# Expert gates as two f16 parts held twice, with one pass of bias products

## The chip, the cores and the metric

The kernel runs on one core of a Trainium2 chip. The metric is the device time of one execution in microseconds, as the median of several runs. The engines: TensorE (PE) multiplies matrices, VectorE (DVE), ScalarE (ACT) and GpSimd (POOL) work on SBUF and PSUM, SyncE (SP) issues the transfers. Each runs its own queue of instructions in order; they wait for each other by semaphores.

## The reference

Input x has the shape (16, 64, 112, 112). In short:

```python
v = _ln_c(x)                                   # norm over the channels
pooled = stack([max(v, axis=1), mean(v, axis=1)], axis=1)
x = x + v * sigmoid(conv3x3(pooled, conv_w) + conv_b)
t = _to_tokens(x)                              # tokens of 64 channels
u = _ln_t(t)                                   # norm of each token
probs = softmax(u @ router_w + router_b)       # 8 experts
top_p, top_i = top_k(probs, 2); top_p /= sum(top_p)
t = t + sum over the 2 of top_p * (u @ expert_w[i] + expert_b[i])
```

The affine steps of both norms and of the gate of the convolution reduce, for a token, to a few numbers: the gate of each expert, the same gate times the token's scale rho, the residual's scale and a mean term.

## The kernel before, in words

The 16 images go as 8 pairs (the two images lie on partitions 0 to 63 and 64 to 127). A pair has 14 steps of 8 image rows, 896 tokens an image. Three stages run at once on three different pairs, and a "round" r is the time in which stage A works on pair r, stage B on pair r - 1 and stage C on pair r - 2. Rounds 2 to 7 have all stages, round 8 has no stage A, rounds 9 and 10 only the rest of stage C. Each engine's order of work is written out by hand in its body(r, ...); the same step appears in each engine's queue.

- Stage A: TensorE centres the rows of x (centre_rows, L444, two groups a step). ScalarE copies the result to xct, squares it and sums; VectorE takes the maximum over the channels (L639).
- Stage B: the router and the gate. Its work has image row as partition (112 partitions). gate() puts one piece of it at each place 2 * step + late of VectorE: root_step (L751, L753, L756: two or more inputs in SBUF) at places 1 to 3 and 7 to 9, half_router at places 12 to 19 for the first half of the tokens and 20 to 27 for the second. At the third and seventh of these eight places stand key (L689) and key_max (L681), at the fourth oh1 (L697) and dl (L699). GpSimd has one or two operations of 896 elements in most steps (router, router_tail), among them e (L1237), that the root step of place 1 waits for, summed_gates (L1216) and scaled_gates (L1222).
- Stage C: the expert mixture in channel form, step v = step - 2. All numbers of a token are first split in bfloat16 parts so that TensorE can move them exactly, turned to rows of the matrix s (turn, L458), and spread over the channels by a matmul against a 0/1 matrix (spread, L465) into four PSUM banks gb. VectorE multiplies six of the eight spread gates by x (scale_unit, L662, gx<-gb,xd), GpSimd two of them (L1148), which ScalarE first copies out of PSUM (L963, gs). experts (L520) multiplies gx by the expert's weights and adds up in PSUM (moe); biases (L514) adds the bias of the chosen experts to the same accumulator. spread_a1 (L504) makes the scale of the residual, GpSimd multiplies it by x (tt, L1173), and VectorE adds tt and moe (finish, L675).

The parts: q holds for a token 18 numbers (8 scaled gates, 8 gates, 2 others). part_one (ScalarE, L942) rounds q to bfloat16, rest_one (GpSimd, L1156) subtracts it from q, part_two (ScalarE, L948) rounds the rest, part_three (GpSimd, L1162) subtracts again. The turn waits for part_three. Expert biases are split in two f16 parts, bh and bl, and each is multiplied with s in a pass of its own.

The order of one step on TensorE, with the calls before each wait on VectorE:

```
spread(v,1) spread_pool(v,1) | expert 5 of v-1 | turn(v+1) | biases(v,0) | expert 0
spread(v,2) spread(v,3) | centre_rows 0 | expert 1, pool expert 0
spread(v,4) spread_pool(v+1,0) | expert 2 | spread_a1(v+1) | biases(v,1) | expert 3
spread(v,5) spread(v+1,0) | centre_rows 1 | expert 4, pool expert 1
```

On VectorE a step is: gate(late=False), scale 1, finish, scale 2, scale 3, maximum, gate(late=True), scale 4, finish, scale 5, scale 0 of v+1, maximum. On GpSimd: scale_unit(v,1), rest_one(v+2), router pieces, scale_unit(v+1,0), scale_x (tt), part_three(v+2). A spread waits until VectorE has read the bank that it writes.

Of the kernel before, what the change touches and what calls it, by code (L numbers as in the profile page):

```python
# [33 lines left out]
E = 8  # L34
P = 128
# [19 lines left out]
SB = 64  # L55
SR = SB + 3 * QN
QG, QB, QA, QM = 0, E, 2 * E, 2 * E + 1
D_PAIR = (0, 1, 3, 0, 1, 3)
# [11 lines left out]
         + tuple(n + "_1" for n in HALF_ROUTER))  # L70
B_POOL = ("lg_0", "bias_0", "lg_1", "bias_1", "m1_0", "m2_0", "qb_0", "qg_0", "m1_1", "m2_1", "qb_1", "qg_1")
B_NORM = ("e1", "e2")
B_ACT = ("sig", "wide_0", "g1_0", "g2_0", "qa_0", "wide2_0", "wide_1", "g1_1", "g2_1", "wide2_1", "qa_1")
GUESS = 0x5F3759DF


def constant_arrays():

    f = np.zeros((P, CC + 3 * W + E + P), np.float32)
# [12 lines left out]
    f[:, o:o + E] = np.arange(E, 0, -1)  # L92
    o += E
    for part in range(3):
        for b in range(2):
            f[b * SB + part * QN + QM, o + b * CH:o + (b + 1) * CH] = -1.0
    g = np.zeros((P, (KT + 2) * P), np.float32)
    for part in range(3):
        for b in range(2):
            row = b * SB + part * QN  # L100
            for k in range(KT):
                for e in range(2):
                    lo = k * P + e * CH
                    g[row + QG + 2 * k + e, lo:lo + CH] = 1.0
            g[row + QA, KT * P + b * CH:KT * P + (b + 1) * CH] = 1.0
    g[:, (KT + 1) * P:] = np.eye(P)
    return f, g


def gated_expert_program(nc, x, conv_w, conv_b, router_w, router_b, expert_w, expert_b, const_f, const_g, out):  # L110
# [3 lines left out]
    with ExitStack() as ctx:  # L114
        def sb(name, shape, dt=F32):
            return ctx.enter_context(nc.sbuf_tensor(name, shape, dt))
# [4 lines left out]
        def sem(name):  # L121
            return ctx.enter_context(nc.semaphore(name))

        cf = sb("cf", [P, CC + 3 * W + E + P])
        cg = sb("cg", [P, (KT + 2) * P], BF16)
        gx = sb("gx", [P, UNITS, 2, HALF])
# [16 lines left out]
        bh = sb("bh", [SR, P], F16)  # L143
        bl = sb("bl", [SR, P], F16)
        cwb = sb("cwb", [W, 18])
# [39 lines left out]
        q = sb("q", [W, H, 2 * QN])  # L185
        res = sb("res", [W, 2, ROWS, 2 * QN])
        parts = sb("parts", [W, 2, ROWS, 2 * SB], BF16)
        s = sb("s", [P, 2, TOK], BF16)
        gs = sb("gs", [P, NP, 2, HALF])
# [9 lines left out]
        conv_out = tm[0:W, 0, 0:2 * H]  # L199
        turn_out = tm[:, 1, :].bitcast(BF16)  # L200

# [23 lines left out]
        rest1 = sem("rest1")  # L225
        part2 = sem("part2")
        part3 = sem("part3")
        turned = sem("turned")
# [11 lines left out]

        FIRST_LOADS, LOADS, BIAS_LOADS = 3 * 16, 5 * 16, 6 * 16
        POOL_SETUP = 5 + 1 + 6 * 5 + 1 + 2

# [16 lines left out]
        def c_at(r, per_step, v, n):  # L260
            return at(r, 2, per_step * STEPS, per_step * v + n)
# [72 lines left out]
        def _(sp):  # L334
# [65 lines left out]
            sp.wait_ge(ld_first, FIRST_LOADS)  # L400
            for part in range(3):
                for b in range(2):
                    row = b * SB + part * QN + QB
                    col = bias_c + b * CH
                    sp.dma_start(cf[row:row + E, col:col + CH], expert_b).then_inc(ld_bias, 16)

# [12 lines left out]
        def _(pe):  # L419
# [41 lines left out]

            def spread(v, k, c, slot):
                for b in range(2):
                    rows = slice(b * SB, b * SB + 3 * QN)
# [416 lines left out]
        def _(act):  # L881
# [168 lines left out]
            def body(r, A, Bp, steps=STEPS, tail=True):  # L1050
                for step in range(steps):
# [26 lines left out]
                    if A:  # L1078
                        square(r, step, 1)
                    if parting:  # L1080
                        part_two(r, v + 2)
                    if Bp and step == 8:
# [21 lines left out]
        def _(pool):  # L1104
# [171 lines left out]
            def body(r, Bp, steps=STEPS, tail=True):  # L1276
                for step in range(steps):
# [49 lines left out]
```

## Time and profile before

| | |
|---|---|
| median of 3 runs | 1491.57 us (1489.61 to 1493.1) |
| profiled execution, its own time | 1497.93 us |
| its span | 1496.1 us |
| TensorE busy | 1402.2 us, 94% |
| VectorE busy | 1268.4 us, 85% |
| ScalarE busy | 1080.0 us, 72% |
| GpSimd busy | 1086.4 us, 73% |
| mean granted clock of TensorE | 0.963 |

The time of a run is the whole execution; the span reaches from the first to the last instruction of the profile. Busy shares are averages over all rounds. A timeline row gives the start in us from the span's start, the duration in us, the engine and line, the operation, what it writes and reads, and in brackets the idle time of the engine before it with what ended it.

### The profile page before, as it was taken

The page shows a single profiled execution, that of the slowest core. Times are in us where ns is not written, and L with a number is a line of the kernel's source. Part 1 is how long each engine was busy: PE and PEld are TensorE (multiplying, and loading weights), DVE is VectorE, ACT ScalarE, POOL GpSimd, SP SyncE. Part 2 cuts the span into 40 slices and gives each one's busy share as a digit, 9 for nine tenths or more (in the row PEclk, how much of TensorE's full clock was granted, in tenths as well). Part 3 has the DMA queues.
Part 4 walks back from the last instruction along what each step waited for, and adds up shares of the span by engine and source line. Part 5 has one row for each costly group of instructions (what it writes and reads, how often), then busy time and mean ns, then how long its engine had stood idle before and what let it go on. Part 6 is the DMA issues. An engine that isn't in the chain of part 4 may idle for free.

```text
span 1496.1 us, 34317 instructions
## 1 busy us (share of the span) xinstructions
PE 1402.2 (94%) x12198; PEld 660.5 (44%) x12198; DVE 1268.4 (85%) x1583; ACT 1080.0 (72%) x4061; POOL 1086.4 (73%) x729
## 2 busy tenths in 40 slices
PE   8854999999999999999999999999999889999998
PEld 8853444444444444444444444444444233333332
DVE  6787889988998889988898889988898788977776
ACT  6667788878887888878888788878888334444432
POOL 5234687868777787877788687876878678887765
PEclk9955999999999999999999999999999899999999
DMA  6442466656666566666656666666665356556563
GB/s 221 125 114 60 138 197 197 203 156 203 190 188 193 178 199 197 185 179 193 185 173 198 186 186 192 177 199 186 195 193 169 101 151 170 173 164 182 165 181 112
DMA packets 85851, 260.04 MB, mean 174 GB/s; under 512 B 13744, under 2 KB 13744, under 8 KB 85680
## 3 DMA queue, kind: packets, MB, share of 16 engines
q1 hardware_dynamic: 85680, 257.85, 57.7%
q8 instruction: 97, 1.59, 0.4%
q14 instruction: 74, 0.61, 0.1%
HBM read 206.41 MB, written 51.38 MB: 172 GB/s over the span
## 4 chain that ended last, share of the span: by engine, by line
PE 69%; DVE 9%; issue 7%; POOL 3%; ACT 3%; DVEq 0%; POOLq 0%; ACTq 0%
PE moe L520 39%; PE gb L465 13%; PE tm L444 8%; DVE gx L662 7%; PE moe L514 4%; PE tm L458 3%; PE tm L504 2%; POOL gx L1148 1%; PE tm L544 1%; POOL tt L1173 1%; ACT a1s L970 1%; ACT sq L919 1%; POOL parts L1162 1%; DVE stats L639 0%; ACT logit_mean L985 0%
## 5 line engine op out<-in xcount | busy, mean ns | idle before, releaser
L662 DVE TENSOR_TENSOR gx<-gb,xd 128x896 f32<-128x896 f32 x672 | 710.7, 1085 | 139.0 <-PE gb L465 135.6
L520 PE MATMUL moe<-gx,wc 128*64 128x448 f32 x3584 | 820.6, 558 | 0.0
L1148 POOL TENSOR_TENSOR gx<-gs,xd 128x896 f32<-128x896 f32 x224 | 486.2, 2170 | 302.1 <-ACT gs L963 291.6
L963 ACT ACTIVATE gs<-gb 128x896 f32<-128x896 f32 x224 | 205.3, 917 | 225.1 <-PE gb L465 225.0
L919 ACT ACTIVATE sq<-xct 112x64 f32<-112x64 f32 x1400 | 338.0, 244 | 8.1 <-DVE early_s L649 2.6
L520 PEld LDWEIGHTS moe<-gx,wc 128*64 128x64 f32 x3584 | 219.2, 137 | 244.0 <-issue 193.3
L465 PE MATMUL gb<-s,cg 54*128 54x448 bf16 x1792 | 261.4, 360 | 40.8 <-DVE gx L662 34.6
L919 ACT ACTIVATION_READ_ACCUMULATOR sq<-xct 112x1 f32 x1400 | 263.7, 188 | 0.0
L1173 POOL TENSOR_TENSOR tt<-xc,a1s 128x896 f32<-128x896 f32 x112 | 236.2, 2109 | 12.2 <-issue 10.5
L465 PEld LDWEIGHTS gb<-s,cg 54*128 54x128 bf16 x1792 | 57.0, 95 | 377.9 <-DVE gx L662 292.6
L444 PEld LDWEIGHTS tm<-rhs,xa 64*112 64x112 f32 x2800 | 175.1, 185 | 29.7 <-issue 11.5
L444 PE MATMUL tm<-rhs,xa 64*112 64x74 f32 x2800 | 171.7, 265 | 11.2 <-ACT logit_mean L904 8.4
L675 DVE TENSOR_TENSOR ot<-moe,tt 128x448 f32<-128x448 f32 x224 | 138.0, 616 | 31.5 <-PE moe L520 30.8
L900 ACT ACTIVATE xct<-tm 112x512 f32<-112x512 f32 x175 | 104.2, 595 | 61.2 <-PE tm L444 55.6
L970 ACT ACTIVATE a1s<-tm,ones 128x896 f32<-128x896 f32 x112 | 112.8, 1007 | 43.5 <-PE tm L504 43.5
L955 ACT ACTIVATE s<-tm 128x896 bf16<-128x896 bf16 x112 | 102.6, 916 | 11.9 <-PE tm L458 7.2
L639 DVE TENSOR_REDUCE stats<-xct 112x8 f32<-112x512 f32 x128 | 86.8, 678 | 18.3 <-ACT logit_mean L904 17.5
L1156 POOL TENSOR_TENSOR res<-q,parts 112x288 f32<-112x288 f32 x112 | 81.2, 725 | 9.7 <-ACT parts L942 9.7
L458 PEld LDWEIGHTS tm<-cg,parts 112*64 112x64 bf16 x1792 | 56.8, 111 | 67.7 <-POOL parts L1162 44.1
L1162 POOL TENSOR_TENSOR parts<-res,parts 112x288 bf16<-112x288 f32 x112 | 83.1, 742 | 0.1
L514 PE MATMUL moe<-s,bh 118*64 118x448 bf16 x448 | 80.8, 354 | 0.0
L639 DVE TENSOR_REDUCE early_s<-xct 112x8 f32<-112x512 f32 x96 | 65.1, 678 | 18.2 <-ACT early_l L904 17.3
(94 smaller groups left out, 1296.7 us busy)
## 6 DMA issues: line engine op xcount, KB each, us to landing
xd<-in_x_dram SPq DMA_DIRECT2D x448, 224.0 KB, 4.0
xa<-in_x_dram SPq DMA_DIRECT2D x112, 448.0 KB, 4.3
xc<-in_x_dram SPq DMA_DIRECT2D x112, 448.0 KB, 4.8
out_dram<-ot SPq DMA_DIRECT2D x112, 448.0 KB, 3.3
gx<-in_const_g_dram SPq DMA_DIRECT2D x1, 384.0 KB, 4.7
cf<-in_const_f_dram SPq DMA_DIRECT2D x1, 332.5 KB, 2.8
gx<-in_L_ffn_expert_w_dram SPq DMA_DIRECT2D x1, 128.0 KB, 4.5
cf<-in_L_ffn_expert_b_dram SPq DMA_DIRECT2D x6, 2.0 KB
```

The lines of the kernel that those rows point to most:

```text
L444: last = pe.matmul(pair[:, b, j, :], xa[chans, step % XA, row * W:(row + 1) * W], rhs1[chans, :], start=True, stop=True)
L465: last = pe.matmul(gb[:, 2 * slot + b, 0:HALF], cg[rows, k * P:(k + 1) * P], s[rows, v % 2, c * HALF:(c + 1) * HALF], start=True, stop=True)
L514: pe.matmul(moe[b * CH:(b + 1) * CH, c, 0:HALF], w[:, b * CH:(b + 1) * CH], s[0:SR, v % 2, c * HALF:(c + 1) * HALF], start=(n == 0), stop= ...
L520: last = pe.matmul(moe[b * CH:(b + 1) * CH, c, 0:HALF], wc[:, k * CH:(k + 1) * CH], gx[:, u, b, :], start=False, stop=(k == KT - 1), skip_ ...
L639: dve.tensor_reduce(to[:, 0, lo + cols.start:lo + cols.stop], xct[:, step % 2, cols, :], AX.X, ALU.max) \
L662: dve.tensor_tensor(gx[:, i, :, :], gb[:, 2 * slot:2 * slot + 2, 0:HALF], xd[:, v % 2, :, c * HALF:(c + 1) * HALF], ALU.mult).then_inc(sca ...
L675: dve.tensor_tensor(ot[:, sl, cols], moe[:, c, 0:HALF], tt[:, sl, cols], ALU.add).then_inc(final, 1)
L919: last = act.activation(sq[:, n, :], xct[:, step % 2, n, :], ACT.Square, accum_out=to[:, 1, lo + n:lo + n + 1])
L963: act.activation(gs[:, j, :, :], gb[:, 2:4, 0:HALF], ACT.Copy).then_inc(gate_out, 1)
L970: act.activation(a1s[:, v % 2, :].rearrange("p (c t) -> p c t", c=2), tm[:, :, 0:HALF], ACT.Identity, bias=ones[:, :], scale=1.0).then_inc ...
L1148: pool.tensor_tensor(gx[:, ND + j, :, :], gs[:, j, :, :], xd[:, v % 2, :, j * HALF:(j + 1) * HALF], ALU.mult).then_inc(scaled_p, 1)
L1173: pool.tensor_tensor(tt[:, sl, :], xc[:, sl, :], a1s[:, sl, :], ALU.mult).then_inc(scaled_x, 1)
```

## The change

Numbers are split in two f16 parts instead of three bfloat16 parts. The 18 numbers of a token are read as two overlapping blocks of 13: the first five scaled gates and the eight gates; then the eight gates again, the last three scaled gates and the two others. So the gates stand twice in each part, and s has 2 x 26 = 52 rows an image instead of 54. The high and the low part of the bias stand at the two copies of the gates in one matrix bw, and one pass of bias products replaces two. part_two and part_three are gone, with res, and the turn waits for rest_one. part_one and rest_one handle 416 elements a partition instead of 288. scaled_gates is two instructions (5 and 3 experts) instead of one. cg, ident, parts and s are f16. Setup loads the expert bias 8 times instead of 6 and builds bw with two products and a sum.

```diff
-QG, QB, QA, QM = 0, E, 2 * E, 2 * E + 1
+G_LO = 5
+QB, QA, QM = G_LO, 2 * E, 2 * E + 1
+BLOCK, AGAIN = QB + E, QB
+PN = 2 * BLOCK
+SR = SB + 2 * PN
...
-        parts = sb("parts", [W, 2, ROWS, 2 * SB], BF16)
-        s = sb("s", [P, 2, TOK], BF16)
+        parts = sb("parts", [W, 2, ROWS, 2 * SB], F16)
+        s = sb("s", [P, 2, TOK], F16)
...
+            tokens = parts[:, v % 2, :, :].rearrange("w j (b k) -> w (j b) k", b=2)
+            return tokens[:, :, n * PN:(n + 1) * PN].rearrange("w t (i k) -> w t i k", i=2)
+
+        def q_blocks(v):
+
+            rows = q[:, v * ROWS:(v + 1) * ROWS, :]
+            return bass.AP(rows.tensor, rows.offset, [rows.ap[0], [QN, 2 * ROWS], [AGAIN, 2], [1, BLOCK]])
...
-                    pe.wait_ge(part3, count)
+                    pe.wait_ge(rest1, count)
...
-                for n, w in enumerate((bh, bl)):
-                    for b in range(2):
-                        pe.matmul(moe[b * CH:(b + 1) * CH, c, 0:HALF], w[:, b * CH:(b + 1) * CH],
-                                  s[0:SR, v % 2, c * HALF:(c + 1) * HALF],
-                                  start=(n == 0), stop=False, skip_group_check=True)
+                for b in range(2):
+                    pe.matmul(moe[b * CH:(b + 1) * CH, c, 0:HALF], bw[:, b * CH:(b + 1) * CH],
+                              s[0:SR, v % 2, c * HALF:(c + 1) * HALF],
+                              start=True, stop=False, skip_group_check=True)
...
-                act.activation(part_of(v, 0), by_part(q[:, v * ROWS:(v + 1) * ROWS, :]), ACT.Copy) \
-                   .then_inc(part1, 1)
-
-            def part_two(r, v):
-                if due(count := c_at(r, 1, v, 1)):
-                    act.wait_ge(rest1, count)
-                act.activation(part_of(v, 1), by_part(res[:, v % 2, :, :]), ACT.Copy).then_inc(part2, 1)
+                act.activation(part_of(v, 0), q_blocks(v), ACT.Copy).then_inc(part1, 1)
...
-            link(pool.tensor_tensor(bl[:, :], bias_base, bh[:, :], ALU.subtract))
+            link(pool.tensor_tensor(bias_base, bias_base, low_row.to_broadcast([SR, P]), ALU.mult))
+            link(pool.tensor_tensor(bh[:, :], bh[:, :], high_sign.to_broadcast([SR, P]), ALU.mult))
+            link(pool.tensor_tensor(bw[:, :], bias_base, bh[:, :], ALU.add))
...
-                pool.tensor_tensor(by_part(res[:, v % 2, :, :]), by_part(q[:, v * ROWS:(v + 1) * ROWS, :]),
-                                   part_of(v, 0), ALU.subtract).then_inc(rest1, 1)
-
-            def part_three(r, v):
-                if due(count := c_at(r, 1, v, 1)):
-                    pool.wait_ge(part2, count)
-                pool.tensor_tensor(part_of(v, 2), by_part(res[:, v % 2, :, :]),
-                                   part_of(v, 1), ALU.subtract).then_inc(part3, 1)
+                pool.tensor_tensor(part_of(v, 1), q_blocks(v), part_of(v, 0), ALU.subtract).then_inc(rest1, 1)
...
-                pool.tensor_tensor(q_tokens[:, rows, QG:QG + E], q_tokens[:, rows, QB:QB + E], wide(rho, rows),
+                rhos = wide(rho, rows)
+                pool.tensor_tensor(q_tokens[:, rows, 0:G_LO], q_tokens[:, rows, QB:QB + G_LO], rhos[:, :, 0:G_LO],
                                    ALU.mult).then_inc(b_pool, 1)
+                pool.tensor_tensor(q_tokens[:, rows, QB + E:QA], q_tokens[:, rows, QB + G_LO:QB + E],
+                                   rhos[:, :, G_LO:E], ALU.mult).then_inc(b_pool, 1)
```

## Rows read from the trace of the kernel before

**Rows 1.** the page's busy time, share of the span and instructions, TensorE's line.
```profile
PE 1402.2 (94%) x12198; PEld 660.5 (44%) x12198; DVE 1268.4 (85%) x1583; ACT 1080.0 (72%) x4061; POOL 1086.4 (73%) x729
```

**Rows 2.** timeline of TensorE, round 4: start, duration (us), line, operation, idle before it.
```profile
598.08 0.55 PE L465 MATMUL gb<-s,cg 54*128 54x448 bf16 x4
...
600.98 0.55 PE L465 MATMUL gb<-s,cg 54*128 54x448 bf16 x4
...
604.36 0.55 PE L465 MATMUL gb<-s,cg 54*128 54x448 bf16 x4 [0.40 <-DVE gx L662]
...
608.92 0.36 PE L514 MATMUL moe<-s,bh 118*64 118x448 bf16 x2
609.11 0.36 PE L514 MATMUL moe<-s,bl 118*64 118x448 bf16 x2
...
610.16 0.55 PE L465 MATMUL gb<-s,cg 54*128 54x448 bf16 x4
```

**Rows 3.** timeline of VectorE, round 4, four of its operations.
```profile
553.92 0.61 DVE L689 TENSOR_TENSOR key<-ge,prio 112x896 bf16<-112x896 bf16 x1
...
601.09 1.10 DVE L689 TENSOR_TENSOR key<-ge,prio 112x896 bf16<-112x896 bf16 x1
...
603.22 1.08 DVE L662 TENSOR_TENSOR gx<-gb,xd 128x896 f32<-128x896 f32 x1
...
607.36 0.61 DVE L697 TENSOR_TENSOR oh<-prio,ge 112x896 bf16<-112x896 bf16 x1
```

**Rows 4.** timeline of GpSimd over the stretch of rows 2.
```profile
600.98 0.72 POOL L1162 TENSOR_TENSOR parts<-res,parts 112x288 bf16<-112x288 f32 x1
...
605.33 2.11 POOL L1216 TENSOR_TENSOR q<-lg,dl 112x896 f32<-112x896 f32 x1
608.89 2.22 POOL L1148 TENSOR_TENSOR gx<-gs,xd 128x896 f32<-128x896 f32 x1 [1.45 <-ACT gs L963]
```

**Rows 5.** timelines of VectorE, GpSimd and TensorE, round 5, step 0.
```profile
644.12 0.39 DVE L753 SCALAR_TENSOR_TENSOR u<-u,e 112x224 f32<-112x224 f32 x1
644.55 2.21 DVE L756 SCALAR_TENSOR_TENSOR p<-u,p 112x224 f32<-112x224 f32 x1
...
644.18 2.33 POOL L1148 TENSOR_TENSOR gx<-gs,xd 128x896 f32<-128x896 f32 x1 [0.84 <-issue]
...
647.82 0.93 PE L465 MATMUL gb<-s,cg 54*128 54x448 bf16 x4 [2.31 <-DVE gx L662]
```

**Rows 6.** groups of instructions, shapes apart: busy us, mean ns, idle before them.
```profile
L1156 POOL TENSOR_TENSOR res<-q,parts 112x288 f32<-112x288 f32 x112 | 81.2, 725 | 9.7 <-ACT parts L942 9.7
...
L948 ACT ACTIVATE parts<-res 112x288 bf16<-112x288 f32 x112 | 48.3, 431 | 0.0
...
L1201 POOL TENSOR_TENSOR lg<-oh,g 112x896 f32<-112x896 bf16 x16 | 27.8, 1736 | 19.3 <-ACT g L1012 19.3
```

**Rows 7.** windows: stretch, length, busy us by engine, granted clock, DMA share, GB/s.
```profile
538.37:544.48 6.11, 6.00 (x63) 2.68 (x62) 5.20 (x6) 5.34 (x24) 6.03 (x4) 1.00 0.55 138
476.27:483.71 7.44, 7.44 (x60) 3.32 (x61) 5.91 (x9) 4.07 (x15) 2.89 (x3) 0.77 0.49 123
```

**Rows 8.** timelines of VectorE and of TensorE, round 8.
```profile
1160.25 2.22 DVE L753 SCALAR_TENSOR_TENSOR u<-u,e 112x224 f32<-112x224 f32 x1
1162.50 2.14 DVE L756 SCALAR_TENSOR_TENSOR p<-u,p 112x224 f32<-112x224 f32 x1
...
1198.84 2.26 DVE L785 SCALAR_TENSOR_TENSOR top<-avm,gap 112x224 f32<-112x224 f32 x1
...
1165.70 0.93 PE L465 MATMUL gb<-s,cg 54*128 54x448 bf16 x4 [4.50 <-DVE gx L662]
```

**Rows 9.** timelines of VectorE and GpSimd, round 4, step 1.
```profile
487.96 0.39 DVE L756 SCALAR_TENSOR_TENSOR r<-u,p 112x224 f32<-112x224 f32 x1
...
485.15 2.10 POOL L1216 TENSOR_TENSOR q<-lg,dl 112x896 f32<-112x896 f32 x1
488.25 2.14 POOL L1148 TENSOR_TENSOR gx<-gs,xd 128x896 f32<-128x896 f32 x1 [1.00 <-ACT gs L963]
```

More of the change, by code:

```diff
@@ L55 @@
 SB = 64
-SR = SB + 3 * QN
-QG, QB, QA, QM = 0, E, 2 * E, 2 * E + 1
+G_LO = 5
[3 more added lines that the diff above has]
+SR = SB + 2 * PN
 D_PAIR = (0, 1, 3, 0, 1, 3)
@@ L70 @@
          + tuple(n + "_1" for n in HALF_ROUTER))
-B_POOL = ("lg_0", "bias_0", "lg_1", "bias_1", "m1_0", "m2_0", "qb_0", "qg_0", "m1_1", "m2_1", "qb_1", "qg_1")
+B_POOL = ("lg_0", "bias_0", "lg_1", "bias_1", "m1_0", "m2_0", "qb_0", "ql_0", "qg_0", "m1_1", "m2_1", "qb_1",
+          "ql_1", "qg_1")
 B_NORM = ("e1", "e2")
@@ L74, with gate_col, part_col @@
 GUESS = 0x5F3759DF
+def gate_col(e):
+    return e if e < G_LO else E + e
+def part_col(col):
+    return col if col < AGAIN else BLOCK + col - AGAIN
 def constant_arrays():
-    f = np.zeros((P, CC + 3 * W + E + P), np.float32)
+    f = np.zeros((P, CC + 3 * W + E + P + 2), np.float32)
     for b in range(2):
@@ L93, in constant_arrays @@
     o += E
-    for part in range(3):
+    f[:, o + P] = 1.0
+    for part in range(2):
         for b in range(2):
-            f[b * SB + part * QN + QM, o + b * CH:o + (b + 1) * CH] = -1.0
+            row = b * SB + part * PN
+            f[row + part_col(QM), o + b * CH:o + (b + 1) * CH] = -1.0
+            low = slice(row + part_col(QB), row + part_col(QB) + E)
+            f[low, o + P], f[low, o + P + 1] = -1.0, 1.0
     g = np.zeros((P, (KT + 2) * P), np.float32)
-    for part in range(3):
+    for part in range(2):
         for b in range(2):
-            row = b * SB + part * QN
+            row = b * SB + part * PN
             for k in range(KT):
@@ L103, in constant_arrays @@
                     lo = k * P + e * CH
-                    g[row + QG + 2 * k + e, lo:lo + CH] = 1.0
-            g[row + QA, KT * P + b * CH:KT * P + (b + 1) * CH] = 1.0
+                    g[row + part_col(gate_col(2 * k + e)), lo:lo + CH] = 1.0
+            g[row + part_col(QA), KT * P + b * CH:KT * P + (b + 1) * CH] = 1.0
     g[:, (KT + 1) * P:] = np.eye(P)
@@ L122, in sem @@
             return ctx.enter_context(nc.semaphore(name))
-        cf = sb("cf", [P, CC + 3 * W + E + P])
-        cg = sb("cg", [P, (KT + 2) * P], BF16)
+        cf = sb("cf", [P, CC + 3 * W + E + P + 2])
+        cg = sb("cg", [P, (KT + 2) * P], F16)
         gx = sb("gx", [P, UNITS, 2, HALF])
@@ L135, in gated_expert_program @@
         bias_base = cf[0:SR, bias_c:bias_c + P]
+        high_sign = cf[0:SR, bias_c + P:bias_c + P + 1]
+        low_row = cf[0:SR, bias_c + P + 1:bias_c + P + 2]
         cg_load = gx_flat[:, 0:(KT + 2) * P]
@@ L143, in gated_expert_program @@
         bh = sb("bh", [SR, P], F16)
-        bl = sb("bl", [SR, P], F16)
+        bw = sb("bw", [SR, P], F16)
         cwb = sb("cwb", [W, 18])
@@ L185, in gated_expert_program @@
         q = sb("q", [W, H, 2 * QN])
-        res = sb("res", [W, 2, ROWS, 2 * QN])
-        parts = sb("parts", [W, 2, ROWS, 2 * SB], BF16)
-        s = sb("s", [P, 2, TOK], BF16)
+        parts = sb("parts", [W, 2, ROWS, 2 * SB], F16)
+        s = sb("s", [P, 2, TOK], F16)
         gs = sb("gs", [P, NP, 2, HALF])
@@ L199, in gated_expert_program @@
         conv_out = tm[0:W, 0, 0:2 * H]
-        turn_out = tm[:, 1, :].bitcast(BF16)
+        turn_out = tm[:, 1, :].bitcast(F16)
         ld_first = sem("ld_first")
@@ L225, in gated_expert_program @@
         rest1 = sem("rest1")
-        part2 = sem("part2")
-        part3 = sem("part3")
         turned = sem("turned")
@@ L239, in gated_expert_program @@
         final = sem("final")
-        FIRST_LOADS, LOADS, BIAS_LOADS = 3 * 16, 5 * 16, 6 * 16
-        POOL_SETUP = 5 + 1 + 6 * 5 + 1 + 2
+        FIRST_LOADS, LOADS, BIAS_LOADS = 3 * 16, 5 * 16, 8 * 16
+        POOL_SETUP = 5 + 1 + 6 * 5 + 1 + 4
         def at(r, first, per, n):
@@ L400, in _ @@
             sp.wait_ge(ld_first, FIRST_LOADS)
-            for part in range(3):
+            for part in range(2):
                 for b in range(2):
-                    row = b * SB + part * QN + QB
-                    col = bias_c + b * CH
-                    sp.dma_start(cf[row:row + E, col:col + CH], expert_b).then_inc(ld_bias, 16)
+                    for first_row in (QB, part_col(QB)):
+                        row = b * SB + part * PN + first_row
+                        col = bias_c + b * CH
+                        sp.dma_start(cf[row:row + E, col:col + CH], expert_b).then_inc(ld_bias, 16)
             body(0, True)
@@ L463, in spread @@
                 for b in range(2):
-                    rows = slice(b * SB, b * SB + 3 * QN)
+                    rows = slice(b * SB, b * SB + 2 * PN)
                     last = pe.matmul(gb[:, 2 * slot + b, 0:HALF], cg[rows, k * P:(k + 1) * P],
@@ L1079, in body @@
                         square(r, step, 1)
-                    if parting:
-                        part_two(r, v + 2)
                     if Bp and step == 8:
@@ L1153, in rest_one @@
                     pool.wait_ge(part1, count)
-                if due(count := c_at(r, 1, v - 2, 1)):
-                    pool.wait_ge(part3, count)
-                pool.tensor_tensor(by_part(res[:, v % 2, :, :]), by_part(q[:, v * ROWS:(v + 1) * ROWS, :]),
-                                   part_of(v, 0), ALU.subtract).then_inc(rest1, 1)
-            def part_three(r, v):
-                if due(count := c_at(r, 1, v, 1)):
-                    pool.wait_ge(part2, count)
-                pool.tensor_tensor(part_of(v, 2), by_part(res[:, v % 2, :, :]),
-                                   part_of(v, 1), ALU.subtract).then_inc(part3, 1)
+                pool.tensor_tensor(part_of(v, 1), q_blocks(v), part_of(v, 0), ALU.subtract).then_inc(rest1, 1)
             def scale_x(r, v):
@@ L1290, in body @@
                         scale_x(r, v + 1)
-                    if parting:
-                        part_three(r, v + 2)
             for step in range(ACT_STEPS, STEPS):
```

3 lines of the change are left out of this document (removed).

## The prediction

> **What bounds the kernel now.** I read the busy shares first, then TensorE's timeline in one steady round, then VectorE's and GpSimd's over the same stretch. TensorE is busy 94% of the span [rows 1], so its work is the first suspect. In the timeline [rows 2] the reader is to see "spread groups" of L465 (four matmuls each) as milestones. A step has two halves. The first, from 598.08 to 604.36, holds the turn; the second, from 604.36 to 610.16, holds the a1 spread; each holds one call of biases(). The second takes 5.80 us with no idle TensorE: this is TensorE's own length of a half. The first takes 6.28 us, and 0.40 us of it is idle until VectorE's gx (L662) is done. So VectorE sets the length of some halves: between the milestones it does three multiplies, one finish, one maximum, and whatever piece of the router gate() puts there. That fixed part is 604.36 - 598.08 minus the router piece. The piece is key and key_max; key starts at 601.09 and the next multiply at 603.22 [rows 3], so the piece is 2.13 us and the fixed part 4.15 us. A half therefore lasts the longer of TensorE's 5.80 us and 4.15 us plus the piece.
>
> The pieces are not constant, and this matters most. key takes 1.10 us at 601.09 and 0.61 us at 553.92 [rows 3]. At 600.98 GpSimd had just begun part_three (0.72 us) [rows 4]; at 553.92 it was idle. Key's end lies about 0.49 us behind part_three's. The same reading explains root_step (L756) at 644.55: 2.21 us where its twin before it took 0.39, because GpSimd's gx began at 644.18 [rows 5]. TensorE then idled 2.31 us. So VectorE operations with two SBUF inputs queue behind a running GpSimd operation. The Trainium skill, "SBUF — State Buffer", section "SBUF: two separate sides", says this of a pair of ports the two engines share: whichever starts first holds it for its whole instruction and the other fully blocks. By that rule a delay of a tenth of a microsecond can cost two; if the two merely shared bandwidth, the collisions below would cost little and the second rival's time would come out. The rows agree with the rule.
>
> **The change, part by part.** *Bias pass.* biases() issues two matmuls in place of four. Consecutive passes start 0.19 us apart (608.92, 609.11) [rows 2], so each half of TensorE drops from 5.80 to 5.61 us: 0.38 us a step, over 112 steps at most 42 us. f16 in place of bf16 I price at nothing: the f16 weights of this pass already run. The spread's 54 rows become 52, also nothing.
>
> *Parts.* ScalarE loses part_two (431 ns) [rows 6] and its part_one grows from 288 to 416 elements, perhaps 0.1 us; ScalarE is rarely late, but in step 6 join_early makes its queue late for the maximum, and there it returns about 0.2 us. GpSimd loses part_three (0.72 us); rest_one grows from 288 to 416 elements. Its row is 725 ns, and the nearest other mixed f32/bf16 row is 1736 ns for 896 [rows 6]. The slope gives 725 + 128 x 1.66 = 938 ns; in proportion it would be 1047 ns. So rest_one is 0.21 to 0.32 us longer; I take 0.25. The turn now waits for rest_one, done some 8 us earlier, instead of part_three, which ran last there: the turn half of step 6, which had to wait for it, takes 6.11 us [rows 7] and falls to 5.61, 0.50 less. scaled_gates becomes two instructions for 896 elements, 0.1 to 0.2 us more twice a round, and falls beside the ge of step 12. Setup gains two bias loads and two small products ahead of a GpSimd that waits for ScalarE: nothing; uncovered it is 1 us.
>
> *One steady round (rounds 3 to 7), 28 halves.* What has slack in VectorE gets the 0.19:
> - 14 halves in full: 2.66 us. Step 6's turn half: 0.50. Five in part (steps 3, 4, 6, 7, 10; VectorE's piece, or GpSimd ahead of it, nearly fills them): 0.60. One (step 12, the split scaled_gates) not at all.
> - The three turn halves with a key beside part_three (steps 9, 11, 13): part_three is gone, but the tt before it ends 0.19 us later against VectorE, so key falls from 1.10 to about 0.68: 0.42 each, 1.28 in all.
> - Losses: the operation behind rest_one is later against VectorE by 0.25 (rest_one) plus 0.19 (a faster turn half). In step 11 summed_gates ended at 607.44, just as oh1 (607.36, 0.61 us) started. Now the milestone also comes 0.41 us sooner: q ends about 0.74 us into oh1's piece, and oh1 takes 1.2: half 6.41 instead of 5.80, a loss of 0.61. In step 7 the same costs 0.21.
> Subtotal: 5.04 - 0.82 = 4.2 us gained.
>
> *Step 0, second half.* Here e (L1237) comes through GpSimd behind rest_one, and VectorE's root_step waits for it. The middle operation (L753) started at 644.12, 0.06 us before gx at 644.18 [rows 5], and escaped. Now e is later by 0.25 and gx earlier by 0.19, so L753 arrives 0.38 us after gx; even with rest_one unchanged it would be 0.13 after. It blocks until gx ends, tt starts, and L756 blocks on tt. Round 8 shows just this: 2.22 and 2.14 us, and TensorE idle for 4.50 instead of 2.31 us [rows 8]. Cost 2.2 us a round.
>
> *Step 1, second half.* L756 started at 487.96, 0.29 us before gx at 488.25, while L751 had already waited for q (485.15) [rows 9]. q is later by 0.25 + 0.19 = 0.44 us: L756 arrives 0.15 us behind gx and blocks: 8.0 us for the half instead of 5.8, 2.2 us. With rest_one only 0.10 us longer it would escape; where the slow clock reaches into the first half of the step, it would too.
>
> *Clock.* After TensorE's idle 2.31 us the granted clock fell to the lower of its two levels (1.2 of 2.4 GHz) for a while: the half 476.27 to 483.71 ran at 0.77 and took 7.44 us, 1.64 more than 5.80 [rows 7]. A second long idle in step 1 brings a second dip, 1.7 us; the longer one of step 0 I put at 0.5 (bounds nothing and 1.7).
>
> Round: 4.2 - 2.2 - 2.2 - 1.7 - 0.5 = -2.4 us, a loss, times five = -12 us.
>
> *The other rounds.* Round 2 has neither collision new: +4. Rounds 9 and 10 have no router: 16 x 0.38 = +6. Round 8 has no maxima and already both collisions; two more of 2 us stand there behind part_three (the one of L785, 2.26 us [rows 8], and a root_step). Without part_three they start about 0.1 to 0.2 us before gx; I count one as gone: 14 x 0.38 less the same small losses, +4, and 2: +6 (bounds 2 and 11). Sum +16.
>
> **Sum.** 16 - 12 = 4 us off the profiled execution: 1497.9 becomes 1494. The profiled one lies 6.4 us above the median of the runs, so the median becomes 1491.6 - 4 = 1488.
>
> **The rivals.**
> 1. Step 1 escapes (rest_one cheaper, or the clock's dip reaches the point where q is placed). Per round 2.2 and 1.7 come back and 0.3 of plain delay stays: +1.2 a round, five times +6: gain 22, time 1470. For it: a margin of 0.15 us made of five terms.
> 2. No new collision at either place, because the queues shift together or blocking is milder: +3.9 a round and 16: gain 35, time 1456; with all pieces hidden, the full 42: 1449. Against it: L753's 0.06 us margin.
> 3. Slower: in step 11 the blocked oh1 pushes dl (L699) behind gx. dl would start 0.27 us before gx (gx is 4.53 us behind the milestone: 604.36, 608.89 [rows 2, 4]; oh1 starts 3.00 behind it, 607.36, and takes 1.2 and a gap, so dl comes at 4.26). If rest_one is 0.27 us dearer still, 1.25 us or more (rows of 13 elements read less well), it blocks: 2.2 us and another dip of 1.7 in five rounds, 19.5 us: 1507. Decided from rest_one at 1.2 us.
> 4. The pass doesn't shorten TensorE (weight load of the experts not covered by one bias matmul). Today it hides under one 0.19 us pass and will have the same cover; the time would be about 1500.
>
> **How the numbers follow.** Forecast 45%, rival 1 25%, rival 2 12%, rival 3 13%, rival 4 and the rest 5%. The forecast's own range is 1480 to 1497 (the clock's terms and round 8). The range for 8 in 10 reaches from 1460, most of the way into rival 2, to 1503. A measurement of this kernel can tell about 0.2%, 3 us. The forecast lies 0.25% below the median, so its 45% split: 22 faster, 12 same, 11 slower. With rivals 1 and 2 faster is 59%, with rival 3 and 4 slower 27%, same 14%.
>
> **What the profile after would show.** One L514 group of 448 matmuls at 353 ns; halves without router work at 5.61 us; the turn no longer waiting; L942 near 540 ns, rest_one near 940. Right or wrong of the collisions: in step 0's second half two root_step operations above 2 us and TensorE idle 4.5; in step 1 one above 2 us, idle near 2.3; key near 0.7, oh1 of step 11 near 1.2. More dips of the clock than one a round confirm the loss. If root_step stays at 0.4 us in step 1, rival 1; if L753 does in step 0 as well, rival 2; a dl above 2 us is rival 3; spacing of 0.38 between the turn and the experts is rival 4.

## The result and the profile after

| | before | after |
|---|---|---|
| median of 20 runs | 1491.65 us | 1499.63 us |
| lowest to highest | 1488.94 to 1497.51 us | 1494.47 to 1502.79 us |
| profiled execution | 1497.93 us | 1497.48 us |
| its span | 1496.1 us | 1495.7 us |
| mean granted clock | 0.963 | 0.953 |

The change makes the kernel slower: the ratio is 1.005, with a 95% interval of 1.0037 to 1.0062. I had forecast 1488 us, 0.25% faster, with 1480 to 1497 as the forecast's own range. The two profiled executions show no such loss (1497.93 and 1497.48): the one of before is higher than all 20 of its timed runs, and the one of after, itself one of the 20, lies 2.15 us below their median.

The page of the kernel after, and its groups of instructions (shapes apart):

```profile
PE 1372.2 (92%) x11750; PEld 639.8 (43%) x11750; DVE 1291.6 (86%) x1583; ACT 1046.1 (70%) x3949; POOL 1052.9 (70%) x635
```

```profile
L1168 POOL TENSOR_TENSOR parts<-q,parts 112x416 f16<-112x416 f32 x112 | 107.7, 962 | 10.2 <-ACT parts L962 10.2
...
L534 PE MATMUL moe<-s,bw 116*64 116x448 f16 x448 | 80.8, 354 | 0.0
...
L962 ACT ACTIVATE parts<-q 112x416 f16<-112x416 f32 x112 | 61.1, 546 | 0.0
...
L704 DVE TENSOR_TENSOR ge<-lg,top 112x896 bf16<-112x896 f32 x16 | 31.3, 1958 | 0.0
```

TensorE has 30 us less to do (1372.2 for 1402.2 in [rows 1]), as the single bias pass promised: one group at 354 ns is left where two stood. rest_one (L1168) takes 962 ns, part_one (L962) 546 ns. The span hardly moved, so some 30 us of new idle time stand in TensorE's queue. One group hints at a place: ge (L704) of the first logits had a mean of 1224 ns before and now has 1958; half of the 11.7 us that it gained is one single operation, shown below.

I read the length of each half between its spread groups, as in the prediction. Here round 3 (us, turn half / a1 half; the steps left out are as step 5):

```
step            0            1          2          3          4          5          6          7          9          11         13
before  5.81/ 8.17  7.40/ 5.79  5.81/8.25  5.81/5.79  5.81/5.79  5.81/5.79  6.11/5.79  6.44/6.09  6.29/5.79  6.28/5.80  6.27/5.79
after   5.64/10.33  8.14/ 7.98  5.62/8.06  5.77/5.61  5.64/5.72  5.62/5.60  5.64/5.64  6.26/6.32  5.80/5.60  5.79/6.48  6.02/5.60
```

Rounds 4 to 7 repeat it, but for what the slow clock touches: the first half of step 1 (7.40 to 8.97 us before, 7.25 to 8.77 after) and, after the change alone, that of step 2 (8.77 in round 5, 7.23 in round 7); and the second half of step 1 is 5.94 us in round 4 after.

Step 0 of round 5 after, on VectorE, GpSimd and TensorE:

```profile
638.16 0.39 DVE L771 TENSOR_TENSOR u<-p 112x224 f32<-112x224 f32 x1
638.59 2.22 DVE L773 SCALAR_TENSOR_TENSOR u<-u,e 112x224 f32<-112x224 f32 x1
640.84 2.14 DVE L776 SCALAR_TENSOR_TENSOR p<-u,p 112x224 f32<-112x224 f32 x1
...
638.23 2.33 POOL L1162 TENSOR_TENSOR gx<-gs,xd 128x896 f32<-128x896 f32 x1 [0.41 <-issue]
640.52 2.21 POOL L1178 TENSOR_TENSOR tt<-xc,a1s 128x896 f32<-128x896 f32 x1
...
644.04 0.93 PE L486 MATMUL gb<-s,cg 52*128 52x448 f16 x4 [4.68 <-DVE gx L682]
```

The reader is to see two root operations above 2 us. L773 starts 0.36 us after gx (638.23) and ends behind it (640.81, gx at 640.56); tt follows gx at once and holds L776. TensorE waits 4.68 us where it waited 2.31 in [rows 5]. Step 1 of the same round, and of round 4:

```profile
657.29 2.23 DVE L776 SCALAR_TENSOR_TENSOR r<-u,p 112x224 f32<-112x224 f32 x1
...
657.13 2.14 POOL L1162 TENSOR_TENSOR gx<-gs,xd 128x896 f32<-128x896 f32 x1 [0.55 <-ACT gs L977]
...
486.10 0.39 DVE L776 SCALAR_TENSOR_TENSOR r<-u,p 112x224 f32<-112x224 f32 x1
...
486.15 2.35 POOL L1162 TENSOR_TENSOR gx<-gs,xd 128x896 f32<-128x896 f32 x1 [0.76 <-ACT gs L977]
```

In round 5 L776 starts 0.16 us after gx and takes 2.23 us; in round 4 it starts 0.05 us before gx and takes 0.39. Before, it had 0.29 us to spare [rows 9]. Step 11 of round 4, where the forecast had a gain and a loss side by side:

```profile
595.93 0.61 DVE L709 TENSOR_TENSOR key<-ge,prio 112x896 bf16<-112x896 bf16 x1
...
601.72 1.29 DVE L717 TENSOR_TENSOR oh<-prio,ge 112x896 bf16<-112x896 bf16 x1
603.05 1.09 DVE L719 SCALAR_TENSOR_TENSOR dl<-oh,lg 112x896 f32<-112x896 bf16 x1
...
600.43 2.11 POOL L1221 TENSOR_TENSOR q<-lg,dl 112x896 f32<-112x896 f32 x1
603.25 2.89 POOL L1162 TENSOR_TENSOR gx<-gs,xd 128x896 f32<-128x896 f32 x1 [0.72 <-ACT gs L977]
```

key is down from 1.10 us [rows 3] to 0.61 (in step 13 it still takes 0.84, behind the end of tt), and oh1 up from 0.61 to 1.29, because q now ends about 0.8 us into it.

Round 8, step 6, is the place that I had not foreseen:

```profile
1234.58 7.05 DVE L704 TENSOR_TENSOR ge<-lg,top 112x896 bf16<-112x896 f32 x1
...
1233.93 0.95 POOL L1168 TENSOR_TENSOR parts<-q,parts 112x416 f16<-112x416 f32 x1
1234.84 1.73 POOL L1191 TENSOR_TENSOR lg<-logit_mean,rho 112x896 f32<-112x896 f32 x1
1236.54 2.12 POOL L1162 TENSOR_TENSOR gx<-gs,xd 128x896 f32<-128x896 f32 x1
1238.60 2.08 POOL L1178 TENSOR_TENSOR tt<-xc,a1s 128x896 f32<-128x896 f32 x1
```

rest_one, lg, gx and tt stand on GpSimd without a gap, and ge, that comes behind rest_one, waits for all four. The windows of rounds 3 to 7 and of round 8, before and then after:

```profile
290.80:1150.00 859.20, 837.10 (x7624) 390.01 (x7624) 763.47 (x955) 723.04 (x3007) 657.95 (x421) 0.99 0.63 188
1150.00:1320.10 170.10, 154.35 (x1096) 53.85 (x1096) 147.96 (x164) 70.86 (x122) 133.88 (x85) 0.97 0.53 152
```

```profile
284.20:1150.70 866.50, 820.26 (x7344) 376.51 (x7344) 781.07 (x955) 701.77 (x2936) 639.50 (x361) 0.98 0.62 186
1150.70:1326.50 175.80, 153.48 (x1038) 52.22 (x1036) 153.65 (x164) 67.01 (x108) 128.22 (x73) 0.93 0.51 147
```

Rounds 3 to 7 are 7.3 us longer and round 8 is 5.7 us longer; the granted clock is lower in both.

### The profile page after: what moved, and what is told of

Same layout as the page of the kernel before. It is cut to its first block, busy times and chain, and to the rows that moved or that the text cites. A ratio compares the mean times of both kernels' runs of the same rounds, so it can differ in the third digit from the quotient of the medians.

```text
span 1495.7 us, 33107 instructions
## 1 busy us (share of the span) xinstructions
PE 1372.2 (92%) x11750; PEld 639.8 (43%) x11750; DVE 1291.6 (86%) x1583; ACT 1046.1 (70%) x3949; POOL 1052.9 (70%) x635
## 4 chain that ended last, share of the span: by engine, by line
PE 65%; DVE 16%; issue 9%; ACT 1%; DVEq 0%; POOL 0%; ACTq 0%; POOLq 0%
PE moe L540 37%; PE gb L486 13%; DVE gx L682 10%; PE tm L465 8%; PE tm L479 2%; PE moe L534 2%; PE tm L525 2%; PE tm L564 1%; DVE u L773 1%; DVE u L771 1%; DVE oh L717 1%; DVE ot L695 1%; DVE early_s L659 0%; ACT sq L939 0%; ACT gs L977 0%
## 5 line engine op out<-in xcount | busy, mean ns | idle before, releaser
L1162 POOL TENSOR_TENSOR gx<-gs,xd 128x896 f32<-128x896 f32 x224 | 491.4, 2194 | 337.2 <-ACT gs L977 317.7
L486 PE MATMUL gb<-s,cg 52*128 52x448 f16 x1792 | 264.2, 363 | 74.9 <-DVE gx L682 66.9
L486 PEld LDWEIGHTS gb<-s,cg 52*128 52x128 f16 x1792 | 56.9, 94 | 416.4 <-DVE gx L682 336.6
L465 PE MATMUL tm<-rhs,xa 64*112 64x74 f32 x2800 | 175.0, 268 | 11.6 <-ACT logit_mean L924 8.4
L1168 POOL TENSOR_TENSOR parts<-q,parts 112x416 f16<-112x416 f32 x112 | 107.7, 962 | 10.2 <-ACT parts L962 10.2
L969 ACT ACTIVATE s<-tm 128x896 f16<-128x896 f16 x112 | 102.6, 916 | 1.6 <-PE tm L479 1.4
L659 DVE TENSOR_REDUCE stats<-xct 112x8 f32<-112x512 f32 x128 | 86.7, 677 | 17.2 <-ACT logit_mean L924 16.4
L479 PEld LDWEIGHTS tm<-cg,parts 112*64 112x64 f16 x1792 | 60.0, 111 | 57.4 <-issue 57.4
L659 DVE TENSOR_REDUCE early_s<-xct 112x8 f32<-112x512 f32 x96 | 65.1, 678 | 19.4 <-ACT early_l L924 18.2
L534 PE MATMUL moe<-s,bw 116*64 116x448 f16 x448 | 80.8, 354 | 0.0
L479 PE MATMUL tm<-cg,parts 112*64 112x112 f16 x1792 | 64.1, 214 | 1.4 <-ACT early_l L924 1.3
```

Of the source, the lines that this page charges most:

```text
L465: last = pe.matmul(pair[:, b, j, :], xa[chans, step % XA, row * W:(row + 1) * W], rhs1[chans, :], start=True, stop=True)
L659: dve.tensor_reduce(to[:, 0, lo + cols.start:lo + cols.stop], xct[:, step % 2, cols, :], AX.X, ALU.max) \
L1162: pool.tensor_tensor(gx[:, ND + j, :, :], gs[:, j, :, :], xd[:, v % 2, :, j * HALF:(j + 1) * HALF], ALU.mult).then_inc(scaled_p, 1)
```

## The experiments

All ratios are against the kernel before, run beside each experiment on the same chip.

**Experiment 1: e ahead of second_gates.** In the body of GpSimd:

```diff
-                    if tail:
-                        router_tail(r - 1, step)
                     if Bp:
                         router(r, step)
+                    if tail:
+                        router_tail(r - 1, step)
```

> The changed kernel, with one order exchanged on GpSimd in step 0: root_of (e, for which VectorE's root step waits) goes ahead of second_gates. Theory of collisions: e comes 1.7 us earlier, both blocked root_step operations of step 0 find GpSimd waiting, the second half of step 0 falls from 10.35 us to between 5.6 and 6.0, TensorE's idle 4.68 us goes and with it the clock's dip behind it (first half of step 1 from 7.3 to 8.8 us down to 5.6). The second half of step 1 stays at 8.0 us. About 7 us in each of six rounds: near 1460 us. Rival (the loss comes from rest_one's length, f16 or the turn, spread over all steps): no change beyond 3 us, 1497 to 1502.

Measured: 1494.28 us, ratio 1.0027 (1.0005 to 1.0049), and the second half of step 0 at 10.12 to 10.16 us. Neither theory's number. Its timeline in step 0 of round 5:

```profile
636.68 1.26 DVE L765 TENSOR_SCALAR p<-e 112x224 int32<-112x224 int32 x1
...
638.41 2.18 DVE L773 SCALAR_TENSOR_TENSOR u<-u,e 112x224 f32<-112x224 f32 x1
640.62 2.14 DVE L776 SCALAR_TENSOR_TENSOR p<-u,p 112x224 f32<-112x224 f32 x1
...
635.52 0.60 POOL L1245 TENSOR_TENSOR e<-stats,powers 112x224 f32<-112x224 f32 x1
636.04 1.77 POOL L1212 TENSOR_TENSOR dl<-oh,g 112x896 f32<-112x896 bf16 x1
638.22 2.12 POOL L1162 TENSOR_TENSOR gx<-gs,xd 128x896 f32<-128x896 f32 x1 [0.40 <-ACT gs L977]
```

e is early indeed (L765 no longer waits for it), but second_gates now runs over the start of the root. L765, one SBUF input and integers, takes 1.26 us for 0.28, and L773 comes 0.19 us after gx again. The order was not the point; that a long operation stands between e and gx was.

**Experiment 2: the sums moved from step 1 to step 2.**

```diff
-                elif step == 1:
-                    summed_gates(r, 1)
                 elif step == 2:
+                    summed_gates(r, 1)
                     scaled_gates(r, 1)
```

> The changed kernel, with summed_gates of the second token half moved on GpSimd from step 1 to step 2, directly ahead of scaled_gates. Theory of collisions: the second half of step 1 falls from 8.0 to about 5.7 us, the dip after it goes too; step 2's second half keeps its 8.06 us, which the convolution sets. Step 0 keeps its 10.35 us. 2.3 us and about 1.5 us of clock in four or five rounds: near 1484 us. Rival: no change beyond 3 us.

Measured: 1477.44 us, ratio 0.9915 (0.9895 to 0.9934). Step 1's second half is 5.60 us in each of rounds 3 to 7, step 2's first half 5.64 everywhere; step 0 keeps 10.3 us. In the medians it gained 22 us where I expected 16. In the traces, rounds 3 to 7 gave 13.7 us (852.7 for 866.4) and round 8 another 11 (164.8 for 175.9), since its step 6 missed the collision this time (5.16 us for 10.52):

```profile
1217.70 1.21 DVE L704 TENSOR_TENSOR ge<-lg,top 112x896 bf16<-112x896 f32 x1
...
1217.93 2.60 POOL L1191 TENSOR_TENSOR lg<-logit_mean,rho 112x896 f32<-112x896 f32 x1
```

ge again started while rest_one ran, 0.69 us into it (0.65 in the changed kernel), but here it was served next, and lg waited instead. The move does not touch step 6, and why ge came first is not shown: this part of the gain is luck.

**Experiments 3 and 4: both moves, on the changed kernel and on the one before.**

> The changed kernel with both moves of GpSimd's work. Theory of collisions: steps 0 and 1 at 5.6 us a half, no dips of the clock in rounds 3 to 7, near 1442 us. Round 8 keeps its own losses. Rival (other bound, as ScalarE or DMA, takes over): halves stay above 5.8 us, above 1470 us.

> The kernel before with both moves. Theory: step 0's second half falls from 8.17 to 5.8 us, the dip behind it goes (7.4 to 9.0 us down to 5.8): 4 us in six rounds, near 1466 us. The difference to the changed kernel with both moves is then what the change is worth with the collisions of steps 0 and 1 out of the way: about 1.6% in favour of the change. Rival: the change itself is worth nothing or costs; the two are within 0.3% of each other.

Measured: 1476.43 us, ratio 0.9912 (0.9896 to 0.9928), and 1489.8 us, ratio 0.9997 (0.9984 to 1.0009). Both fell short for the reason of experiment 1: step 0's second half is 10.15 and 7.95 us. In experiment 4, too, second_gates ran over the root's first operation (0.83 us), and its last, 0.18 us behind gx, took 2.17. I had expected 1.6% between the two kernels and measured 13.4 us, 0.9%: the one still has a double stall, the other a single one, so they don't stand on equal ground.

**Experiments 5 and 6: e alone in step 0.** The repair of experiment 1, on both kernels:

```diff
-                if step == 0:
+                if step == 1:
                     second_gates(r, 1)
-                elif step == 1:
-                    summed_gates(r, 1)
                 elif step == 2:
+                    summed_gates(r, 1)
                     scaled_gates(r, 1)
```

> The changed kernel; on GpSimd e (root_of) now stands alone between rest_one and gx in step 0, second_gates is moved to step 1 and summed_gates with scaled_gates to step 2. In the run with e ahead of second_gates e came early, but second_gates then ran over VectorE's first root operation (L765 took 1.26 us for 0.28), and L773 was behind gx again. Theory of collisions: with no GpSimd operation between e and gx, L765 starts at once, L773 and L776 end before gx; step 0's second half falls from 10.3 to 5.6 us, no dip follows (step 1's first half 5.6), step 1's second half stays under 6.0. Against the run with the sums alone moved (1477 us) that is 7 us in five rounds and some in round 8: near 1436 us. Rival (TensorE's idle in step 0 has another cause, such as waiting for ScalarE's squares): that half stays above 8 us and the time near 1477 us.

> The kernel before with the same three moves. Theory: step 0's second half falls from 8.17 to 5.8 us, step 1's first half from 7.4 to 5.8: about 4 us in each of six rounds, near 1467 us. The distance to the changed kernel with these moves is what the change is worth without the collisions of steps 0 and 1: by my terms some 30 us, 2%. Rival (the change gives nothing of its own): both within 5 us.

Measured: 1433.65 us, ratio 0.9604 (0.9586 to 0.9621), and 1471.32 us, ratio 0.9853 (0.9836 to 0.9869). Step 0 of round 5 in experiment 5, and the windows of its rounds 3 to 7:

```profile
619.24 0.27 DVE L765 TENSOR_SCALAR p<-e 112x224 int32<-112x224 int32 x1
619.54 0.39 DVE L771 TENSOR_TENSOR u<-p 112x224 f32<-112x224 f32 x1
619.97 0.39 DVE L773 SCALAR_TENSOR_TENSOR u<-u,e 112x224 f32<-112x224 f32 x1
620.39 0.39 DVE L776 SCALAR_TENSOR_TENSOR p<-u,p 112x224 f32<-112x224 f32 x1
...
618.12 0.55 POOL L1245 TENSOR_TENSOR e<-stats,powers 112x224 f32<-112x224 f32 x1
620.77 2.14 POOL L1162 TENSOR_TENSOR gx<-gs,xd 128x896 f32<-128x896 f32 x1 [2.10 <-ACT gs L977]
```

```profile
284.30:1100.10 815.80, 802.00 (x7344) 368.91 (x7344) 751.50 (x955) 701.05 (x2936) 637.39 (x361) 1.00 0.65 198
```

All four root operations run at their own pace; the last starts 0.38 us ahead of gx (620.77) and ends as gx starts. The second half of step 0 is 5.61 us, step 1 is 5.64 and 5.77, and no dip of the clock is left in these rounds: the window has 1.00 where the changed kernel had 0.98. Five rounds take 815.8 us instead of 866.5. In experiment 6 the same two halves are 5.79 and 5.81 us, as expected. With the collisions of steps 0 and 1 out of the way on both sides, the change is worth 1471.3 - 1433.7 = 37.7 us, 2.6%. The bias pass alone could give 42 at most; part of the 37.7 comes from the halves with key, which were 6.27 to 6.29 us with part_three and are 5.79 to 6.02 without it. Round 8 keeps its own stalls in both and takes the same time, 163.7 us.

**Experiment 7: new parts, old speed of TensorE.** A second bias pass against zero weights:

```diff
+        bz = sb("bz", [SR, P], F16)
...
-                for b in range(2):
-                    pe.matmul(moe[b * CH:(b + 1) * CH, c, 0:HALF], bw[:, b * CH:(b + 1) * CH],
-                              s[0:SR, v % 2, c * HALF:(c + 1) * HALF],
-                              start=True, stop=False, skip_group_check=True)
+                for n, w in enumerate((bw, bz)):
+                    for b in range(2):
+                        pe.matmul(moe[b * CH:(b + 1) * CH, c, 0:HALF], w[:, b * CH:(b + 1) * CH],
+                                  s[0:SR, v % 2, c * HALF:(c + 1) * HALF],
+                                  start=(n == 0), stop=False, skip_group_check=True)
...
+            link(pool.memset(bz[:, :], 0.0))
```

> The changed kernel with a second bias pass against zero weights (the values stay the same), so TensorE is as slow as before while the parts are the new ones. Halves without collisions go back to 5.80 us. Theory of collisions, by arrival: L773 comes 0.36 us after gx in the changed kernel, minus 0.19 is still 0.17 after: step 0's second half stays at about 10.5 us. In step 1 L776 comes 0.16 after, minus 0.19 is 0.03 before: it escapes, 6.0 us. Near 1505 us. Rival (the faster TensorE alone brings the double stall, not the longer rest_one): step 0's second half back at 8.2 us, near 1491 us.

**Experiment 8: old parts, new speed of TensorE.** The product with the low part of the bias is left out:

```diff
-                for n, w in enumerate((bh, bl)):
+                for n, w in enumerate((bh,)):
```

> The kernel before with one bias pass: the product with the low part of the bias is left out. TensorE is faster by 0.19 us a half, all parts are as before. Theory of collisions: L753 came 0.06 us before gx; now gx comes 0.19 sooner, so it is 0.13 behind and blocks: step 0's second half 10.3 us. In step 1 the margin of 0.29 falls to 0.10: it escapes, about 6.0 us. Near 1483 us. Rival (the longer rest_one is the whole cause): step 0's second half near 8.0 us, near 1468 us.

Measured: 1493.38 us, ratio 1.0002 (0.9992 to 1.0012), and 1489.2 us, ratio 0.9972 (0.9961 to 0.9983). Step 0 of round 5, first in experiment 7 (its lines are two or three further down), then in experiment 8, and last its step 1:

```profile
643.85 2.21 DVE L775 SCALAR_TENSOR_TENSOR u<-u,e 112x224 f32<-112x224 f32 x1
646.09 2.15 DVE L778 SCALAR_TENSOR_TENSOR p<-u,p 112x224 f32<-112x224 f32 x1
...
643.68 2.13 POOL L1165 TENSOR_TENSOR gx<-gs,xd 128x896 f32<-128x896 f32 x1 [0.60 <-issue]
```

```profile
638.23 2.26 DVE L753 SCALAR_TENSOR_TENSOR u<-u,e 112x224 f32<-112x224 f32 x1
640.52 2.15 DVE L756 SCALAR_TENSOR_TENSOR p<-u,p 112x224 f32<-112x224 f32 x1
...
656.39 0.39 DVE L756 SCALAR_TENSOR_TENSOR r<-u,p 112x224 f32<-112x224 f32 x1
...
638.11 2.14 POOL L1148 TENSOR_TENSOR gx<-gs,xd 128x896 f32<-128x896 f32 x1 [0.65 <-issue]
...
656.48 2.31 POOL L1148 TENSOR_TENSOR gx<-gs,xd 128x896 f32<-128x896 f32 x1 [0.79 <-ACT gs L963]
```

In experiment 7 the root's second operation comes 0.17 us after gx (643.85, 643.68), in experiment 8 0.12 us (638.23, 638.11); I had put 0.17 and 0.13. Both have the double stall, about 10.16 us for the half. Round 7 of experiment 7 is the exception, with 8.41: there gx began later, L775 started 0.12 us ahead of it (991.58, 991.70) and took 0.39. So either part of the change is enough for the double stall. Step 1 escapes in rounds 3 to 7 of both, at 5.88 to 5.96 us: in experiment 8 by 0.09 us. It takes both parts to lose that one. Experiment 7 also shows that the types cost TensorE nothing, as I had put: its halves without a collision are 5.79 to 5.81 us as before, with f16 for bf16 and 52 rows for 54. In experiment 7 the total was 12 us better than I expected: the key halves keep 5.81 us instead of the 6.28 of before, since part_three is gone, and round 8 fell to 164.3 us. In experiment 8 it was 6 us worse: the turn, still behind part_three, took 6.30 us in step 6 and 6.63 in step 7, and round 8 stayed at 170.3.

**Experiments 9 and 10: round 8 eased,** on the changed kernel, and with the moves of experiment 5:

```diff
-                elif step == 6:
+                elif step == (7 if r == PAIRS else 6):
                     logits_scaled(r, 1)
-                elif step == 7:
+                elif step == (8 if r == PAIRS else 7):
                     logits_biased(r, 1)
```

> The changed kernel; in round 8 alone logits_scaled of the second token half goes from step 6 to 7 on GpSimd and logits_biased from step 7 to 8. Theory: in step 6 of round 8 rest_one, lg, gx and tt stand on GpSimd without a gap, VectorE's ge (L704) waits 7.05 us for all of them, and TensorE's long idle brings dips of the clock into step 7. With lg gone GpSimd has a gap, ge takes about 1 us, the half falls from 10.52 to about 5.2 us and round 8 from 175.9 to about 165: near 1489 us, so that round 8 is more than the whole loss of 8 us. Rounds 3 to 7 stay as they are. Rival (round 8 is slow for its clock, or the wait goes on to another operation): round 8 within 3 us of 175.9, time within 3 us of 1499.

> The changed kernel with e alone in step 0, second_gates in step 1, both sums in step 2, and round 8 eased as in the run beside this. Against e alone without round 8 eased (1433.7 us) theory gives 10 us less, near 1424 us, with round 8 at 153 to 156 us instead of 163.7 and no dip of the clock after round 2. Rival: round 8 keeps above 160 us.

Measured: 1489.33 us, ratio 0.9973 (0.996 to 0.9987), and 1424.54 us, ratio 0.9549 (0.9533 to 0.9566). ge of experiment 10 in round 8, and the window of that round:

```profile
1173.31 1.26 DVE L704 TENSOR_TENSOR ge<-lg,top 112x896 bf16<-112x896 f32 x1
```

```profile
1100.10:1253.60 153.50, 144.76 (x1040) 51.02 (x1038) 141.56 (x164) 66.89 (x108) 128.45 (x73) 1.00 0.59 169
```

ge takes 1.26 us, the half 5.16, and round 8 153.5 us. In experiment 9 ge takes 1.25 us, the same half 5.16, and round 8 166.1 us, 9.8 us less than in the changed kernel. Experiment 10 is the best version: 67 us below the kernel before, and its four runs lie within 0.4 us, where those of the changed kernel spread over 8.

## Why the prediction was wrong, step by step

Gains and losses in the spans, round by round: I had +4 for round 2 and what lies ahead of it, -12 for rounds 3 to 7, +6 for round 8 and +6 for rounds 9 and 10, 4 us in all. Measured are +6.6, -7.3, -5.7 and +6.8, 0.4 us in all. So round 8 alone was 11.7 us worse than I had it, and the rest 8.1 us better.

- **The bias pass, right.** Halves without a collision are 5.60 to 5.64 us (5.61 forecast). Rounds 9 and 10 gave 6.8 us (6 forecast).
- **Parts, right.** rest_one takes 962 ns (938 put, 1047 the bound), part_one 546 (540). The turn half of step 6 is 5.64 (5.61 forecast).
- **Step 0, right.** 10.35 us for 8.17: a cost of 2.18 (2.2 forecast). Experiments 7 and 8 show that the faster TensorE and the longer rest_one each suffice, as the arrival times had it, and experiment 5 that the half falls to 5.61 us when these operations are clear of gx.
- **Step 1, right.** 7.99 us in four of five rounds (8.0 forecast), escape in round 4 by 0.05 us. My margin of 0.15 was 0.16 in round 5.
- **key and oh1, right in sign.** 5.80, 5.79, 6.02 for the three key halves (5.87 forecast); step 11's second half 6.48 (6.41); step 7's 6.32 (6.30).
- **Clock, right in kind, too high in size.** In rounds 3 to 7 the first halves of steps 1 and 2 lie above their length at full clock (5.81 us before, 5.62 after) by 9.6 us in all before and by 18.0 after: 8.4 us of loss where I had 11. That and the escape in round 4, 2 us, are the whole difference between the 12 us that I had for these rounds and the 7.3 measured; the terms that are left come to a loss of 0.9 us where I had 1.0. In round 2, 2.5 of the 6.6 us come from its step 2 (8.30 and 8.72 us before, 6.11 and 8.45 after), much of which ran at the lower clock; I had no term for it. So 4 to 5 of the 8.1 us in my favour are luck.
- **The first step that failed: round 8.** I put 6 us of gain (bounds 2 and 11) by counting stalls that would go, and a new wait at nothing without looking for one. It cost 5.7. Two stalls of 2 us did go (the turn half of step 3 is 5.18 us for 7.39, that of step 4 5.41 for 7.40), but in step 6 a new one arose (the second half is 10.52 us for 5.36), and with the slow clock behind it steps 7 and 8 together took 28.6 us for 22.2. I had followed VectorE's margins through rounds 3 to 7, and for round 8 only those that stood there already. Experiment 9 gives the size: 9.8 us in round 8, 10.3 us in the medians (1499.6 to 1489.3), more than the whole loss of 8. What it left of round 8 is a gain of 4.0 us on the kernel before (166.1 for 170.1), inside my bounds.
- **The second: the distance of the profiled execution to the median.** I carried 6.4 us over unchanged. The median of before held (1491.65), but the changed kernel's profiled execution lies 2.15 us below its median: 8.5 us of the error of 12. Spans compared with spans, I was 3.6 us off, but only because the rest hid most of round 8. The trace of before was not a typical one: its mean clock was 0.963, and of the 62 runs of this kernel beside the experiments the ten with 0.963 or 0.964 took 1495.8 to 1497.3 us, the other 52, with 0.965 to 0.969, 1488.2 to 1494.4.

Rival 1 (step 1 escapes) holds for one round of five in the trace; rival 2 is excluded, by rounds and by experiments 7 and 8; rival 3 did not occur: dl started 0.20 us before gx (603.05, 603.25) in step 11. Rival 4 named the time that was measured, about 1500, but by chance: its mechanism is excluded, as the single pass did shorten the halves to 5.60 to 5.64 us.

What stays open: why the changed kernel's runs spread over 8 us. They fall into two sets of ten, 1494.5 to 1498.7 and 1500.6 to 1502.8 us, and the median lies in the gap between them. The seven with a mean clock of 0.950 all belong to the upper set, but so do three with 0.953. Margins of 0.05 us, as in round 4, can fall either way from run to run, which would fit: experiment 9 leaves rounds 3 to 7 as they are, and in its trace round 4 did not escape (7.98 us), there was more of the lower clock, and these rounds took 870.0 us for 866.4. But only one execution of the changed kernel was traced, from the lower set, and I did not show it. Nor is it shown what makes some runs of the kernel before spend more time at the lower clock, as the traced one did.

## What to carry to other kernels

When two engines share something that is held for a whole operation, do not price a change by busy time alone: list for each operation of the one how far it starts ahead of the other's next one, and see which margins the change uses up. Here two tenths of a microsecond, saved on the bounding engine or added on GpSimd, moved such operations past each other and cost two microseconds each. Do it for the irregular rounds too, look for stretches in which one engine has no gaps, and before you judge a change, move the work that collides: the same change lost 0.5% in the one order and is worth 2.6% in the other. And compare a profiled execution with profiled executions, not with medians, and look by its mean clock whether it is a typical one.

## What the runs showed of the hardware

- Tenths of a microsecond decide: a root operation that started 0.05, 0.06 or 0.09 us ahead of gx took 0.39 us (after, round 4; [rows 5]; experiment 8, step 1), one that started 0.12 us behind it took 2.26 (experiment 8, step 0).
- A waiting VectorE operation is not always served next. L773 waited for one gx alone (2.22 us), and ge (L704) in round 8 of experiment 2 for rest_one alone (1.21 us); the same ge in the changed kernel waited for rest_one, lg, gx and tt in a row, 7.05 us. What decides this is not shown. The Trainium skill, "SBUF — State Buffer", section "SBUF: two separate sides", has it that whichever starts first holds the shared ports for its whole instruction and the other fully blocks. The single waits agree (2.22 us behind a gx of 2.33); the 7.05 us reach past the end of the one instruction behind which ge came.
- An operation with one SBUF input can be held as well: L765 (tensor_scalar) took 1.26 us for 0.28 beside second_gates in experiment 1, while the 224 maxima (L659) of that trace all kept 0.67 to 0.69 us, 147 of them with a GpSimd operation running as they started.
- GpSimd is held in turn: gx took 2.89 us instead of some 2.15 beside dl in step 11 of the changed kernel (603.25).
